# Moving rotated-row stores out of the slots that transfer maxima, and one PSUM copy a slot earlier, in a fused attention and feed-forward kernel

## The reference

```python
x = x + attention(layernorm(x), Wq, Wk, Wv, Wo)   # 32 query heads, 8 key heads, head size 16
x = x + swiglu(layernorm(x), W_gate, W_up, W_down) # hidden width 1376

# attention, for each key head and its 4 query heads:
q, k = rope(q), rope(k)
att = q @ k.T / 4, masked causally
out = softmax(att) @ v
```

## Time and profile before

| | |
|---|---|
| median of 3 runs | 773.08 us (770.94 to 773.19) |
| profiled execution | 772.49 us, of which the span of the profile is 770.8 us |
| phase 1, to the first matmul of phase 2 | 369.6 us |
| TensorE matmul | 737.8 us, 96% of the span |
| VectorE | 445.2 us, 58% |
| ScalarE | 333.8 us, 43% |
| GpSimd | 241.9 us, 31% |
| mean granted TensorE clock | 0.989 |

### The profile page before, as it was taken

How to read it: one execution, slowest core, us unless ns; L and a number is a source line. 1 busy time by engine, 2 the same in 40 slices (tenths; PEclk the granted TensorE clock), 3 DMA queues, 4 the chain that set the end, 5 groups by cost and what they waited for, 6 DMA issues and landing times.

```text
span 770.8 us, 12186 instructions
## 1 busy us (share of the span) xinstructions
PE 737.8 (96%) x4149; PEld 502.4 (65%) x4164; DVE 445.2 (58%) x1136; ACT 333.8 (43%) x646; POOL 241.9 (31%) x467
## 2 busy tenths in 40 slices
PE   5889999999999999998999999999999999999998
PEld 4645444554444543443788888888888888788886
DVE  6897789888987889997355443234232333231212
ACT  4337678767976778667343222111121111111111
POOL 4257885688658774556000000000000000000000
PEclk9869999999999999999999999999999999999999
DMA  7337587234434455530592103211014020030001
GB/s 272 98 108 250 182 280 239 67 87 125 119 96 130 142 179 151 160 99 29 174 310 72 42 14 118 88 59 51 14 48 142 27 82 27 0 110 1 1 0 55
DMA packets 74759, 81.86 MB, mean 106 GB/s; under 512 B 8864, under 2 KB 58528, under 8 KB 74496
## 3 DMA queue, kind: packets, MB, share of 16 engines
q1 hardware_dynamic: 73408, 79.98, 32.7%
q10 hardware_dynamic: 1296, 1.18, 0.5%
HBM read 57.02 MB, written 33.36 MB: 117 GB/s over the span
## 4 chain that ended last, share of the span: by engine, by line
PE 51%; DVE 0%; issue 0%; DVEq 0%
PE bank L1578 35%; PE ps_y L1630 15%; PE bank L1617 1%; DVE x_in L1560 0%; DVEq L1559 0%
## 5 line engine op out<-in xcount | busy, mean ns | idle before, releaser
L929 DVE CUSTOM_DVE_ANT_0 ps_s<-ps_s,mask_row 128x512 f32<-128x512 f32 (+1 forms) x360 | 192.1, 583 | 36.6 <-PE ps_s L1188 34.0
L792 ACT ACTIVATE probs<-ps_t 128x512 f32<-128x512 f32 (+1 forms) x352 | 178.2, 560 | 68.6 <-PE ps_t L1222 68.3
L1535 DVE TENSOR_TENSOR h<-h,bank 128x512 f32<-128x512 f32 (+1 forms) x44 | 30.2, 687 | 212.8 <-PE bank L1578 211.6
L1188 PE MATMUL ps_s<-k_rows,q_rows 96*128 96x256 bf16 (+3 forms) x512 | 141.0, 309 | 5.7 <-DVE m_raw L929 2.9
L1222 PE MATMUL ps_t<-q_rows,k_rows 98*128 98x512 bf16 (+1 forms) x352 | 126.9, 364 | 4.4 <-DMA q_rows<-m_t 2.4
L240 POOL TENSOR_TENSOR var_eps<-mean_var,eps 128x1 f32<-128x1 f32 x16 | 3.0, 189 | 281.7 <-DVE mean_var L235 281.7
L1473 ACT ACTIVATE h<-bank 128x512 f32<-128x512 f32 (+1 forms) x44 | 26.3, 597 | 145.2 <-PE bank L1578 145.2
L1235 PE MATMUL ps_o<-probs,v_ones 128*32 128x512 f32 (+3 forms) x1024 | 82.0, 438 | 3.4 <-POOL probs L693 1.1
L693 POOL TENSOR_SCALAR_AFFINE_SELECT probs<-probs 128x512 f32<-128x512 f32 x128 | 83.4, 652 | 0.0
L1479 ACT CAST h_hi<-h 128x512 fp32r<-128x512 f32 (+1 forms) x44 | 27.3, 620 | 126.5 <-DVE h L1535 126.5
L1188 PEld LDWEIGHTS ps_s<-k_rows,q_rows 96*128 96x128 bf16 x512 | 48.2, 100 | 47.8 <-DVE m_raw L929 22.3
(11 more groups left out here) (167 smaller groups left out, 1366.1 us busy)
## 6 DMA issues: line engine op xcount, KB each, us to landing
scratch_o<-o_sb SPq DMA_DIRECT2D x31, 256.0 KB, 2.4
q_rows<-scratch_q_parts SPq DMA_DIRECT2D x32, 192.0 KB
x_in<-in_x SPq DMA_DIRECT2D x16, 256.0 KB, 4.0
q_rows<-scratch_q_parts SPq DMA_DIRECT2D x32, 128.0 KB
o_in<-scratch_o SPq DMA_DIRECT2D x64, 64.0 KB
inverse<-scratch_inverse SPq DMA_DIRECT2D x64, 64.0 KB
x_res<-in_x SPq DMA_DIRECT2D x16, 256.0 KB, 2.7
out<-x_in SPq DMA_DIRECT2D x16, 256.0 KB, 2.1
```

What stands on the lines that cost most here:

```text
L792: nc.scalar.activation(probs[:, g % 2, heads * u:heads * (u + 1), CHUNK_AT[c]:CHUNK_AT[c + 1]], ps_t[:, pos % S_BANKS, 0:heads * CHUNK_N[c ...
L929: taken = nc.vector.tensor_tensor_reduce(out=head, in0=head, in1=mask_row[:, T - width:T], scale=1.0, scalar=LOWEST, op0=ALU.add, op1=ALU. ...
L1188: mm = nc.tensor.matmul(bank[:, place], q_rows[r][0:ROWS, j, P * q:P * (q + 1)], k_rows[r][0:ROWS, 0:width], start=(place == 0), stop=(mas ...
L1535: nc.vector.tensor_tensor(h[0:m, r], h[0:m, r], bank[units["up", f] % BANKS][0:m, :], ALU.mult).then_inc(h_ready, 1)
```

## The change

Two constants and the condition that belongs to the second. `LO_SLOT` maps a slot of ScalarE to the tile whose upper parts it copies; SP stores that tile in the slot after. `LAST_O` maps a slot of VectorE in the last pass to the group whose output it takes out of `ps_o`; the changed condition in ScalarE's loop leaves out the same two copies as before.

```diff
-LO_SLOT = {7: 0, 13: 1, 16: 2, 23: 3, 27: 4}
+LO_SLOT = {7: 0, 13: 1, 14: 2, 22: 3, 26: 4}
...
-LAST_O = {26: 5, 30: 6}
+LAST_O = {26: 5, 29: 6}
...
-                    if i == PV_EVACUATE and n >= 1 and (has_next or slot not in LAST_O):
+                    if i == PV_EVACUATE and n >= 1 and (has_next or g - 1 not in LAST_O.values()):
```

## The result

The changed kernel takes 773.44 us (median of 20 runs, 772.25 to 775.86); the kernel before, run between them on the same chip, 771.97 us (20 runs, 769.47 to 774.13). The ratio is 1.0022, with a 95% interval of 1.0012 to 1.0032. So the change costs 1.5 us by the medians, 1.7 by the ratio. That is inside the 0.3% that I had called no difference, but the interval leaves 1 out: it is a small loss, where a small gain was forecast.

The account below looks back on a forecast made before the run. TensorE, busy 96% of the span, was taken as the bound, with time to gain only where it idles in phase 1. First edit +0.35 and second -1.1 made -0.75, say -0.8: 773.08 to 772.3 us, range 769.6 to 774.0.

Parts of the forecast that it names:

- Pass 0, slot 25: Transfer of maxima there: ScalarE copy 0.49 sooner, but second weight copy (0.6) behind the stores; +0.1 us, bounds -0.3, +0.5.
- Pass 0, slot 17: Transfer of maxima there: SP has no gap, so the new order changes nothing; 0 us, bounds -0.75 and +0.3.
- Pass 2, slot 17: Transfer there, issued as before but behind rows, lands 0.46 to 0.89 later and TensorE waits; +0.45 us, bounds 0, +0.9.
- Pass 2, slot 25: Largest stall, 1.28 us, stays: earlier copy (-0.49) is offset by the second Wo load behind the stores (+0.47); 0 us.
- Pass 1, slot 29: Transfer of maxima there comes 0.49 us sooner, so the matmul's stall of 0.17 goes; -0.2 us.
- ScalarE: Exponentials of slots 15, 23 and 27, delayed by the moved copy, stay hidden, with 0.1 us left at slot 23.
- Rival C: Exponentials behind ScalarE's moved copy end too late, nine places losing 0.4 us each; +3.6, 775.9 us; chance 0.06.
- The second edit: End of phase 1: group 6's output copied in VectorE's idle time, so barrier and phase 2 come sooner; -1.1 us.
- rival B: At the barrier: the second edit's gain is not passed on, leaving only +0.35 us, 773.4 us; chance 0.1.
- Rival A: Stores caused the stalls after slots 17, 25 and 29; moving them removes these, 3.0 us, giving 769.0 us; chance 0.14.
- The sum: Whole kernel: first edit +0.35 (bounds -1.3, +1.5) and second -1.1 make -0.75, say -0.8 us.

Follow-up runs that it names:

- the kernel with the stores last: Changed kernel, but SP issues the stores of tiles 2 to 4 at the end of their slot, behind weight copy and Wo loads; 771.35 us, ratio 0.9973.
- the kernel with tile 3 alone: Kernel before with only tile 3 moved (ScalarE's copy in slot 22 instead of 23); 773.90 us, ratio 1.0016.
- the kernel with the transfers first: Kernel before plus the second edit, with SP storing tiles 0, 2, 3 and 4 right behind the transfers of maxima; 768.63 us, ratio 0.9939.

## Why the prediction was wrong

**Pass 0, slot 25: this step failed.** I put +0.1, with bounds of -0.3 and +0.5; the runs show 1.4 us (1.6 less 0.2 of idle matmul, means of eight profiles each). The step saw the fact that mattered: the second weight copy stood in SP's idle time and would stand behind the stores. It priced it as one issue of 0.6 on SP, less 0.49 for the ScalarE copy, and as far as the issue goes that is right: in the changed kernel the transfer comes 0.18 later (5.69 for 5.51), and over the two sets no later at all. What it gave no row to was the second half of its own sentence, the 688 KB "moved just before the rows", for which it allowed 0.4 (from +0.1 to the bound of +0.5). A row was there to be had: in the kernel before, the engines moved 226 GB/s at a share of 0.73 from 119 to 122 us. At that rate 688 KB are 2.3 us of all of them; 0.8 (0.27 of three microseconds) was free; the estimate would have been 1.5 us, and the arrival moved by 1.4. This is hindsight and depends on the stretch taken: for 117 to 122 us, with a share of 0.80 and 271 GB/s, it comes to 1.1. The Trainium skill (DMA: Bandwidth & Descriptors, Queues, rings and completion order) says that what one engine issues goes through one ring on each DMA engine and is taken from it in order; by that the packets of a small transfer start behind those of the large copy. The trace agrees: its data comes 1.4 us later behind the copy and hardly depends on its own issue, and its first packet begins 3.1 us after the issue instead of 2.2. I had weighed only the section on one DMA's receipt, and this one speaks against the change.

**Pass 0, slot 17: bound reached.** Forecast 0, bound +0.3 for just this reason (the weight copy of slot 15 behind the stores). The idle matmul at slot 20 went from 0.66 to 1.00; over eight profiles with tile 2 moved it is 0.95 on the mean, over eight with it where it was, and the stores ahead of the transfer, 0.64. So +0.3, though the two sets overlap (0.70 to 1.27 and 0.44 to 0.99). That it is the weight copy, as the bound had it, is not shown: the kernel with the stores last has the copy ahead of them again and still idles 1.24 there. This stays open. The long issue of 1.35 did not come back, but another DMA of the queue took 1.18 to issue.

**Pass 2, slot 17: right in size, by a reading that was not.** Forecast +0.45; the matmul at 268.20 idles 0.26, slot 19 is 0.32 longer, and over the eight profiles with tile 2 moved it is 0.66 longer on the mean (0.3 to 0.9). Of the eight with tile 2 and its stores where they were, seven show no such idle time; the kernel with tile 3 alone idles 0.59 there, and I have no cause for it. But in the kernel before the transfer was not just in time. The weight load at 265.96 has 0.62 of idle time before it, and so has one for which nothing was late (timeline of PEld of the kernel before):

```profile
275.65 0.10 PEld L1222 LDWEIGHTS ps_t<-q_rows,k_rows 98*128 98x128 bf16 x1 [0.62 <-issue]
```

So 0.62 is what stands there behind products with v in any case, and only what is above it is lateness (0.14 of the 0.76 at slot 28 of pass 0). By the events of the transfer's semaphore in the trace, it landed 2.00 us after its issue, not 2.42, and 0.4 before TensorE came for it. By the same events it takes 1.93 to 2.01 with the stores right ahead in seven profiles (2.93 in the one with tile 3 alone), and 2.62 to 3.37 with rows right ahead in the eight. The difference is larger than the 0.46 to 0.89 that I took, and the 0.4 of slack that I did not see takes part of it back. The rule of the Trainium skill on receipts, cited in the prediction (DMA: Bandwidth & Descriptors, Anatomy of one DMA), finds no support here: the transfer lands sooner behind the stores, not later.

**Pass 2, slot 25: right.** Forecast 0 and a stall of 1 us or more: 1.05 (it was 1.28). **Pass 1, slot 29: forecast -0.2, worth nothing.** The wait of 0.17 went, and slot 31 of pass 1 is 0.24 shorter, but slot 0 of pass 2 is 0.24 longer: what was saved is lost again in the next slot. The same pair stands in four kernels in which this tile and its stores were not moved. The profile of before also has 0.33 in slot 17 of pass 3 that no other profile has in full, so that much of any difference from it is chance.

**ScalarE: right.** Timelines of ACT and PEld of the kernel after, pass 2, slots 23 and 24 (before: the earlier trace rows):

```profile
276.94 1.09 ACT L753 COPY r_top<-rot 128x1024 bf16<-128x1024 bf16 x1
277.89 1.62 ACT L792 ACTIVATE probs<-ps_t 128x512 f32<-128x512 f32 x3
...
278.59 0.10 PEld L1222 LDWEIGHTS ps_t<-q_rows,k_rows 98*128 98x128 bf16 x1
```

The exponential starts behind the copy at 277.89, and the third transposed score at 278.59 has no wait ahead of it. Rival C is out, also by the kernel with the stores last, which keeps this order and gains.

**The second edit: right,** 5.72 to 4.60 for a forecast of 1.1; rival B is out. The exchange on VectorE came as forecast: counted from the last transposed score TensorE goes on 1.2 us sooner and ends its products 1.1 us sooner. But the ratios to the kernel before give the edit alone 0.33% and 0.34%, 2.6 us each time, and the traces only 1.1 at its place. The intervals reach down to 0.15%, 1.2 us, so the two just meet. Whether the edit brings more than its place shows stays open.

**Rival B's number** of 773.4 is what was measured, 773.44, but by luck: its mechanism, a second edit that is not passed on, did not occur.

**Rival A** named the right thing for the wrong edit. As put, the stores would leave the slots and the stalls go; they stayed. But that the queue of SP ahead of the transfers caused them is shown by the kernel with the transfers first, in which all of them are gone. That it reaches 768.6 where A said 769.0 is partly luck, since A counted 0.3 of refilling for each stall and no run shows any. My argument against it, that a new order does not shorten SP's list, was true of the change and not of the kernel: part of what stood ahead of the transfer need not stand there.

**The sum** by the runs: first edit 1.4 + 0.3 + 0.66 = +2.4 (by its median alone +2.2), second -1.1, together +1.3; measured +1.5. With the 2.6 that the times give the second edit it would be about 0, so the agreement is no proof. The forecast had +0.35 for the first edit; of the 2.0 that are missing, 1.3 are in the one term, slot 25 of pass 0, 0.3 in slot 17 of pass 0, and 0.2 each in pass 1 and in slot 17 of pass 2. The 773.44 itself lies inside the range of 769.6 to 774.0 only because the kernel before, 773.08 in three runs, was 771.97 in twenty; the change was forecast as -0.8 and came out as +1.5. The forecast's own range was also added up wrongly: the bounds of the two edits with half a microsecond on either side give 770.0 to 774.6, not 770.9 to 773.4.

## What to carry to other kernels

When a queue of DMAs is put in another order, list, for each small transfer that someone waits for, the bytes issued in the few microseconds ahead of it, not only the issues, and read the share of the DMA engines there. A bulk copy in the idle time of the queue is free only as long as it stays there. And rather than move bulk transfers to other slots, put the urgent small one ahead of them: here this shortened the slots of phase 1 by 2.6 us in the trace, and with the second edit the kernel was 4.5 us faster by the medians. When idle time before an instruction is read as lateness, look first what idle time stands there when nothing is late.

## What the runs showed of the hardware

**A bulk copy holds up what is issued behind it.** While the 16 packets of 44 KB of one copy ran, 49 packets began in two microseconds instead of 586, and the small transfer seven issues behind the copy came 1.4 us later.

**The issue and the landing make up for each other.** Over the sixteen profiles of the table SP issued the same transfer between 5.0 and 6.6 us into the stretch, and it took 2.1 to 4.8 us to be there; the sum stood at 8.7 to 9.5 without the copy in the way and at 10.0 to 11.0 with it. A duration "from issue to landing" of a small transfer is no property of the transfer.

**The clock after a short idle.** TensorE got 1.2 GHz for 3.4 us soon after an idle time of 1.86 or 1.88 us at the barrier, in 2 of 11 profiles; after 0.5 us in none of 7. It costs 1.5 us where it comes. Whether the idle time is its cause is not shown. The Trainium skill (TensorE: Matmul & The Clock Gate, HAM oscillation — how this bites in real kernels) warns of longer idle times than these; the two stretches came without one. Filling the idle time moved the ratios little: by 0.1 to 0.2% where the first edit is in, from -0.16% to +0.03% in the kernel before, and not at all where only the second edit is in or the transfers are first. These ratios are from different series, and their intervals are as wide.

**The clock before the slots begin.** The table of busy time for 33 to 40 us, of the kernel before:

```profile
33.00:40.00 7.00, 4.79 (x20) 3.99 (x20) 4.28 (x8) 4.08 (x7) 4.58 (x5) 0.52 0.53 148
```

and of the changed kernel in its second series:

```profile
33.00:40.00 7.00, 3.37 (x24) 2.29 (x24) 4.62 (x9) 3.20 (x6) 5.47 (x5) 0.95 0.49 140
```

The same work ahead of the first slot gets 1.2 GHz in one execution and 2.4 in another, and the first slot starts at 53.8 us in the one and at 52.2 in the other. Over 129 runs of the kernel before in the series of the experiments, those with a mean granted clock of 0.987 take 775.1 us on the mean (20 runs), of 0.989 773.7 (42), of 0.991 772.9 (27), of 0.993 771.8 (31). So 3 us of spread come with the clock, which is more than either edit: a change of this size can only be judged by the place in the trace, repeated over several profiles, and by medians of many runs.
